# Row maxima on tiles of 128 queries that cross chunk borders, earlier queries, and another order of expert work behind the attention

## What is computed

```python
x = x + conv3x3(group_norm(x, 32), weight)              # 64 -> 64 channels, 10% of the weights are not zero
t = tokens(x)                                           # 8 x 3136 x 64
n = layer_norm(t)
q, k, v = n @ Wq.T + bq, n @ Wk.T + bk, n @ Wv.T + bv
t = t + softmax(q @ k.T / 8) @ v                        # over all 3136 keys of the image
n = layer_norm(t)
p = softmax(n @ gate_w + gate_b)                        # 16 experts
top_probs, top_idx = top_k(p, 2); top_probs /= top_probs.sum()
t = t + sum(top_probs[j] * (silu(n @ w1[e]) * (n @ w2[e])) @ w3[e] for j, e in the two chosen)
```

## Time and profile before

| | |
|---|---|
| median of 3 runs | 2943.6 us (2940.9 to 2945.2) |
| the profiled execution, its own time | 2947.36 us |
| its span, first to last instruction | 2945.6 us |
| mean granted TensorE clock | 0.958 |
| TensorE (PE) busy | 2612.0 us, 89% |
| weight loads (PEld) | 1663.2 us, 56% |
| VectorE (DVE) | 1928.1 us, 65% |
| ScalarE (ACT) | 1300.6 us, 44% |
| GpSimd (POOL) | 1020.2 us, 35% |

### The profile page before, as it was taken

The page is one execution under the profiler, slowest core; times in us unless marked ns, Lnnn a source line. Parts: engine busy times, 40 slices in busy tenths (PEclk is TensorE's granted clock), DMA queues, the critical chain, the costliest instruction groups (busy, mean ns, idle before and its releaser), DMA issues.

```text
span 2945.6 us, 47190 instructions
## 1 busy us (share of the span) xinstructions
PE 2612.0 (89%) x14013; PEld 1663.2 (56%) x14013; DVE 1928.1 (65%) x5389; ACT 1300.6 (44%) x2985; POOL 1020.2 (35%) x1093
## 2 busy tenths in 40 slices
PE   4899989999999999999999999999999999987772
PEld 2455555565656566565656656565655656554661
DVE  4577676766676676767776676767776766763432
ACT  1344444454444444454444545454444545443441
POOL 2022014200343045412452136321552136445656
PEclk8899999999999999999999999999999999997775
DMA  2133101111211122111212122111211112112332
GB/s 61 32 84 75 37 25 43 42 38 29 61 51 47 39 57 59 50 50 37 70 48 53 41 53 65 53 47 39 62 50 48 34 39 62 43 50 68 96 92 48
DMA packets 226462, 153.00 MB, mean 52 GB/s; under 512 B 100144, under 2 KB 216624, under 8 KB 226224
## 3 DMA queue, kind: packets, MB, share of 16 engines
q1 hardware_dynamic: 192112, 98.97, 12.7%
q0 software_dynamic: 31456, 48.03, 6.9%
q10 hardware_dynamic: 2656, 2.98, 0.4%
HBM read 83.92 MB, written 65.27 MB: 51 GB/s over the span
## 4 chain that ended last, share of the span: by engine, by line
PE 57%; DVE 17%; issue 7%; POOL 2%; ACT 1%; DMA 1%; SPq 1%; ACTq 0%; POOLq 0%; DVEq 0%
PE ps_o L1378 14%; PE ps_m L1341 8%; PE ps_s L1364 7%; DVE max_part L1041 5%; PE ps_s L1366 5%; PE ps_x L1522 5%; PE ps_z L1537 3%; PE ps_z L1404 3%; PE ps_z L1507 2%; PE ps_s L1522 2%; POOL got L728 2%; PE ps_y L1457 1%; PE ps_x L1530 1%; PE ps_y L1441 1%; DVE up L1196 1%
## 5 line engine op out<-in xcount | busy, mean ns | idle before, releaser
L1041 DVE TENSOR_REDUCE max_part<-ps_m 112x1 f32<-112x448 f32 x1568 | 950.7, 620 | 624.7 <-PE ps_m L1341 607.5
L886 ACT ACTIVATE prob<-ps_s 128x448 f32<-128x448 f32 x1400 | 751.7, 541 | 889.5 <-PE ps_s L1366 874.6
L1341 PE MATMUL ps_m<-k_a,q_a 128*112 128x448 f32 (+2 forms) x1792 | 611.3, 372 | 70.6 <-DVE max_part L1041 56.6
L1378 PE MATMUL ps_o<-prob,v_s 128*64 128x448 f32 x2800 | 629.6, 558 | 0.0
L1364 PE MATMUL ps_s<-q_a,k_a 128*128 128x448 f32 x1400 | 590.0, 421 | 18.6 <-issue 12.7
L707 POOL DMA_INDIRECT sorted_x<-xn,slot x448 | 433.0, 967 | 244.6 <-issue 197.5
L1366 PE MATMUL ps_s<-q_b,k_a 128*128 128x448 f32 x1400 | 512.1, 366 | 0.0
L728 POOL DMA_INDIRECT got<-sorted_y,slot x448 | 427.3, 954 | 186.4 <-issue 123.0
L746 POOL TENSOR_TENSOR ln_s<-ln_s,minus_half 112x4 f32<-112x4 f32 x56 | 57.9, 1035 | 1246.8 <-DVE ln_s L951 1086.0
L1341 PEld LDWEIGHTS ps_m<-k_a,q_a 128*112 128x112 f32 x1792 | 305.0, 177 | 280.4 <-DVE max_part L1041 162.5
L1364 PEld LDWEIGHTS ps_s<-q_a,k_a 128*128 128x128 f32 x1400 | 264.9, 189 | 208.1 <-issue 178.8
(11 more groups left out here) (184 smaller groups left out, 2944.1 us busy)
## 6 DMA issues: line engine op xcount, KB each, us to landing
fx<-sorted_x SPq DMA_DIRECT2D x43, 384.0 KB
sorted_y<-fy SPq DMA_DIRECT2D x49, 320.0 KB, 3.0
fx<-sorted_x SPq DMA_DIRECT2D x50, 256.0 KB
xh<-in_x SPq DMA_DIRECT2D x96, 126.0 KB, 2.7
sorted_x<-fy POOLq DMA_DIRECT2D x28, 320.0 KB, 6.0
sorted_x<-xn,slot POOLq DMA_INDIRECT x448
got<-sorted_y,slot POOLq DMA_INDIRECT x448
x_now<-in_x SPq DMA_DIRECT2D x112, 56.0 KB, 2.3
```

The lines of the kernel that those rows point to most:

```text
L886: a.activation(prob[(at.n * KEY_TILES + i) % PROBS][:], ps_s[(at.n * KEY_TILES + i) % 2][:, 0:CHUNK], ACT.Exp).then_inc(s["p_ready"], 1)
L1041: v.tensor_reduce(max_part[:, m % PER, m // PER:m // PER + 1], ps_m[m % 2][0:TILE, 0:CHUNK], AX.X, ALU.max).then_inc(s["max_red"], 1)
L1341: done = t.matmul(ps_m[m % 2][0:TILE, first:last], q_a[:, bass.ds(n % QUERIES, 1), j * TILE:(j + 1) * TILE].rearrange("p a c -> p (a c)"), ...
L1378: t.matmul(ps_o[side:side + CHANNELS, 0:CHUNK], v_s[u % 2][:, i, :], prob[(n * KEY_TILES + i) % PROBS][:], start=(i < 2), stop=(i >= KEY_T ...
```

## The change

1. **Maxima.** A query tile is now 128 wide. Three fit a chunk (`FULL`), and the fourth reaches over the border: the last 64 queries of an even chunk and the first 64 of the next odd one. Its seven passes run with the even chunk, so an odd chunk has 21 passes and an even one 28 (the last one's fourth tile has 64 queries): 4 x 28 + 3 x 21 = 175 for an image. The tables follow: 28 passes keep `MAXIMA`, 21 take one in each of steps 0 to 20 (`MAXIMA_FEW`), or two in steps 0 to 3 and one up to 16 in bodies with routing; there `max_total` comes at step 21, `shift` at 22. Bodies ahead of an odd chunk are those with c = 0, 2, 4.
2. **Queries** of chunk n + 2 come at step 7 in every body, since the crossing tile needs them in the same body. `q_a` gets a fourth buffer.
3. **Routing** of a group works on arrays of that group's tiles alone (28, 16, 12), and the zeros go.
4. **Behind the attention.** The body n = 56 has 50 steps: `post` and routing in the first 25 with no pairs, then the two combines at 25 and 28 and the five pairs from 26 on in the form of the later bodies. Image 7's pairs are in slices of four: 4, 4, 4, 4, 4, 2 and 4, 4, 4, 4, 2, so eleven bodies instead of nine, each with one chunk combined.

The core of the diff:

```diff
+LONE_PAIRS = 4
+GROUPS = [Group(image, 0, CHUNKS, 0, PAIRS) for image in range(BATCHES - 1)]
+GROUPS.append(Group(BATCHES - 1, 0, FIRST_PART, 0, LONE_PAIRS))
+GROUPS.append(Group(BATCHES - 1, FIRST_PART, CHUNKS - FIRST_PART, 2 * GROUPS[-1].pairs, LONE_PAIRS))
...
-COMBINE_AT_LAST, COMBINED_AT_LAST = (0, 3), (2, 5)
+COMBINE_AT_LAST, COMBINED_AT_LAST = (KEY_TILES, KEY_TILES + 3), (KEY_TILES + 2, KEY_TILES + 5)
...
-QUERIES = 3
+QUERIES, QUERIES_LOW = 4, 3
...
 MAXIMA = (1, 2, 2, 2) + 15 * (1,) + (2, 2, 2)
-MAXIMA_ROUTING = (2, 2, 2, 2, 1, 2, 1, 1, 1, 2, 1, 1, 1, 2) + 7 * (1,)
-MAX_TO = 22
+MAXIMA_FEW = 21 * (1,)
+MAXIMA_ROUTING = (2, 2, 2, 2) + 13 * (1,)
+MAX_TO, MAX_TO_FEW = 22, 21
+ASK_AT = 7
...
+def passes(n):
+
+    return BOTH + CHUNKS * (n % CHUNKS % 2 == 0)
...
+def maximum_of(n, m):
+
+    if n == 0:
+        return divmod(m, FULL + 1)
+    many = FULL * (CHUNKS - 1)
+    if m < many or passes(n) == BOTH:
+        return m // FULL, m % FULL
+    return (m - many, FULL) if m < many + CHUNKS - 1 else (CHUNKS - 1, m - many - CHUNKS + 1)
...
-        self.beside = self.n <= ALL
+        self.beside = self.n < ALL
...
-        self.ask_at = 18 if c and self.routes is None else 17
+        self.ask_at = ASK_AT
+        self.max_to = MAX_TO_FEW if passes(self.n + 1) == BOTH else MAX_TO
...
+    def steps(self):
+
+        return 2 * KEY_TILES if self.n == ALL else KEY_TILES
...
-    bodies = range(ALL + 1, TURN) if at.n < TURN else range(TURN, EXPERTS_END)
+    bodies = range(ALL, TURN) if at.n < TURN else range(TURN, EXPERTS_END)
...
             def maxima(n, u, which):
 
                 for m in which:
+                    before = passes_before(n) + m
+                    kb, j = maximum_of(n, m)
                     if m == 0:
                         pe.wait_ge(s["qa_ready"], ONE + n + 1)
+                    if j == FULL and kb == 0 and n % CHUNKS < CHUNKS - 1:
+
+                        pe.wait_ge(s["qa_ready"], ONE + n + 2)
...
-                v.tensor_tensor(picks[:, :, group.part], pick1[:, :, group.part], pick2[:, :, group.part], ALU.add)\
+                v.tensor_tensor(by_expert(b, picks), pick1[:, :, group.part], pick2[:, :, group.part], ALU.add)\
```

More of the change, by code:

```diff
@@ L138, with passes_before, queries_of @@
 LAST_GROUP = KEY_TILES // GROUP * GROUP - GROUP
-assert sum(MAXIMA) == TILES and sum(MAXIMA_ROUTING) == TILES
 assert 0 < GIVING < PER and FILLED <= KEY_TILES - OWN
-SHIFT = 23
+WIDE = 128
+FULL = CHUNK // WIDE
+BOTH = FULL * CHUNKS
+def passes(n):
+    return BOTH + CHUNKS * (n % CHUNKS % 2 == 0)
+def passes_before(n):
+    return sum(passes(k) for k in range(n))
+def maximum_of(n, m):
[5 more added lines that the diff above has]
+    return (m - many, FULL) if m < many + CHUNKS - 1 else (CHUNKS - 1, m - many - CHUNKS + 1)
+def queries_of(n, j):
+    c = n % CHUNKS
+    first = c % QUERIES * CHUNK + j * WIDE + (CHUNK - FULL * WIDE) * (c % 2)
+    return slice(first, first + (CHUNK - FULL * WIDE if c == CHUNKS - 1 and j == FULL else WIDE))
 def wait_apart(engine, sem, value):
@@ L289, in expert_steps @@
             if 0 <= k - behind < len(pairs):
-                steps.append((1 + 4 * place, name) + pairs[k - behind])
+                steps.append((at.steps() - KEY_TILES + 1 + 4 * place, name) + pairs[k - behind])
     return steps
@@ L882, in body @@
                 experts = expert_steps(at)
-                for i in range(KEY_TILES):
+                for i in range(at.steps()):
                     if at.attends:
@@ L1250, in body @@
                         next_queries(at.n + 2)
-                    if i == MAX_TO and at.ahead:
+                    if i == at.max_to and at.ahead:
                         max_total(at.n + 1)
@@ L1311, in _ @@
                     next_queries(place - 1)
+                reduces(0, block[3:4])
                 if place < CHUNKS:
@@ L1348, in shift @@
                 pe.wait_ge(s["maxneg_ready"], ONE + n + 1)
-                for j in range(PER):
-                    last = t.transpose(ps_y[:, j * TILE:(j + 1) * TILE],
-                                       max_neg[:, j:j + 1].to_broadcast([TILE, 128]), ident[0:TILE, 0:TILE])
+                part = CHUNK - FULL * WIDE
+                full = [(j, slice(0, WIDE)) for j in range(FULL)]
+                tiles = [(FULL, slice(WIDE - part, WIDE))] + [(FULL + 1 + j, here) for j, here in full] if n % CHUNKS % 2 \
+                    else full + [(FULL, slice(0, part))]
+                first = 0
+                for j, here in tiles:
+                    many = here.stop - here.start
+                    last = t.transpose(ps_y[:, first:first + many], max_neg[here, j:j + 1].to_broadcast([many, 128]), ident[here, here])
+                    first += many
                 last.then_inc(s["shiftT_done"], 1)
@@ L1479, in variance, with routed @@
                     t.matmul(ps_y[:, 1:2], pair_mean[:], gn_e[:], start=True, stop=True).then_inc(s["gn_var_done"], 1)
-            flat_picks = picks[:].rearrange("p e t -> p (e t)")
+            def routed(b, weights):
+                many = EXPERTS * GROUPS[b].tiles
+                return t.matmul(ps_y[0:TILE, 0:many], weights[:], picks[:].rearrange("p e t -> p (e t)")[:, 0:many], start=True, stop=True)
             def route_total(b):
```

121 lines of the change are left out of this document (65 added, 56 removed).

## The result

The changed kernel takes 2900.7 us, the median of 4 runs (2893.4 to 2906.9), against 2944.4 for the kernel before beside it: ratio 0.985, 95% interval 0.982 to 0.988. The forecast was 2868.6 with a range up to 2900, so the direction was right and the size was not: 44 us instead of 75. The experiments ran in four batches, each on a chip of its own and beside the kernel before: e1 to e4 (2943.3 us for the kernel before), a0 and e5 to e7 (3258.7), a1 and f1 to f3 (2943.4), g1 to g4 (2944.6).

The account below looks back on a forecast made before the run. TensorE was taken to set the pace, VectorE holding it up in places. Passes -64 and queries -5, times 0.9, gave -62; with the tail's -13, -75 off the 2943.6 median gave 2868.6 us, own range 2850 to 2885, with near rivals 2840 to 2900.

Parts of the forecast that it names:

- Passes of c = 0, 2, 4: Seven passes fewer in bodies of chunks 0, 2, 4: -4.0, -2.4, -2.1 us, 8.5 an image, -64 in all.
- weight loads cost nothing: Passes loading 128 instead of 112 weight columns: put at nothing, since streaming paces; 18 us if that cover were gone.
- Queries at step 7: Query work moved from step 18 (17): nothing on TensorE, about 0.2 us gained in chunks 1, 3, 5, 6, -5 in all.
- The upper bound of +14 us: Worst case for the queries' move: 54 bodies each 0.25 us late at turned2, nothing gained at step 20.
- The shift: Row-maxima transposes: 64-row pieces not costed; a second reduce under 0.2 us in eight bodies put at nothing.
- Lead-in: First image's start: one pass in four moves behind tokens and queries; put at nothing.
- Tail: Routing and pairs behind the attention: earlier slots, 24 gathers left instead of 40; -14, taken as -13 us.
- signs of being wrong: Chunk 0 body gaining under 2 us, attention clock under 0.97, or more than 32 gathers left behind the pairs.
- signs of being right: Among them: image stretch 335 to about 325 us, chunk 0 4 us shorter, 2 and 4 by 2 to 2.5, others under 0.5.
- TensorE alone paces: Rival: every VectorE wait that goes reappears at hid, xn or the POOL norms; 2904 us (2890 to 2912), chance 0.16.
- The rival of the clock: Rival: missing passes leave gaps, the clock is lowered for longer, kernel slower; 2950 to 2980 us, middle 2960, chance 0.03.

Follow-up runs that it names:

- e1: Kernel before with only the queries moved to step 7 in every body: 2961.4 us against 2943.3, ratio 1.007.
- e4: Changed kernel with the lead-in's fourth passes ahead of turned keys and statistics as before, except where chunk 1's queries are needed: 2891.4 us, ratio 0.983.
- a0: Changed kernel itself again, unaltered, as control on the slow chip: ratio 1.005 to the kernel before.
- e5: Changed kernel with each shift made by four equal 128-row transposes, no 64-row piece, on the slow chip: ratio 1.004 to the kernel before.
- e7: Changed kernel with old lead-in order, four equal transposes per shift, and double passes of steps 19 and 20 at 6 and 14; slow chip, ratio 0.998.
- a1: Changed kernel itself again, unaltered, as control of its batch: 2899.7 us, ratio 0.985 to the kernel before.
- f1: Changed kernel with each shift made by four equal 128-row transposes, no 64-row piece: 2889.2 us, ratio 0.982, beside a control of 2899.7.
- f3: Changed kernel with double passes of steps 19, 20 at 9, 13, last expert codes at step 23, equal-transpose shift, old lead-in order: 2853.3 us, ratio 0.970.
- g1: Kernel before with the double passes of steps 19 and 20 moved to 9 and 13, queries still at step 18: 2938.0 us, ratio 0.998.
- g4: f3 with tables per body: c = 1, 5, 6 move only step 20's double, to 9; first image as in the changed kernel: 2864.2 us, ratio 0.974.
- e3: Changed kernel with the old order behind the attention, image 7's pairs in slices of five: 2912.9 us, ratio 0.989.

## Why the prediction was right and wrong

- **Passes of c = 0, 2, 4**: forecast -4.0, -2.4, -2.1, measured -3.35, -2.26, -2.03, in spite of a shift that cost 0.1 to 0.25 more. Right, body by body. That weight loads cost nothing here was right as well: step 9 takes 2.35 or 2.36 us with either width.
- **Queries at step 7**: forecast -0.2 us in each of c = 1, 3, 5, 6, -5 in all; alone it measured +18. This is the step that failed. The forecast counted q_b on VectorE and took "TensorE's part is the same work elsewhere: nothing". e1 shows +0.6, +0.7, +0.3 and +0.8 in these bodies. The work was the cover of VectorE's reduce, and q_b's leaving step 20 gained nothing there (3.38 us both times). The upper bound of +14 us came from the 0.25 us at turned2. In the changed kernel turned2 waits 1.2 to 1.4 us for q_b in ten bodies of images 1 and 2 (in image 1 of before 0.6 to 0.9 us for the tokens), and 0.2 us in four later ones; the bound is still below the 18 measured.
- **The shift**: never costed, that is, put at nothing without a reason. The forecast weighed only the width of a weight load in the passes; the 64-row transposes in the diff cost about 10 us (f1).
- **Lead-in**: forecast at nothing, "in work that is there anyway". It cost 5.4 us, and the old order gives back 4.4 (e4's trace): the one pass in four had filled part of the wait for the normalised values, which grew from 1.64 to 4.25 us.
- **Tail**: forecast -13; the stretch behind the last score is 13.0 shorter, and undoing it costs 12 to 13 (e3). POOL, then DVE and PE, in the tail of the changed kernel, against the earlier trace rows:

```profile
2679.15 1.14 POOL L765 DMA_INDIRECT got<-sorted_y,slot  x1 [16.87 <-DVE t_out L1269]
2689.27 0.96 POOL L744 DMA_INDIRECT sorted_x<-xn,slot  x1 [0.30 <-issue]
...
2726.82 0.95 POOL L765 DMA_INDIRECT got<-sorted_y,slot  x1 [7.85 <-DMA sorted_y<-fy]
...
2859.20 0.98 POOL L765 DMA_INDIRECT got<-sorted_y,slot  x1 [3.01 <-DMA sorted_y<-fy]
...
2888.28 0.93 POOL L765 DMA_INDIRECT got<-sorted_y,slot  x1 [0.30 <-issue]
```

```profile
2662.39 0.43 DVE L1126 TENSOR_TENSOR ln_c<-ln_c,ln_s 112x256 f32<-112x256 f32 x1 [7.90 <-POOL ln_s L783]
...
2663.75 0.98 PE L1513 MATMUL ps_y<-ident,xn 112*128 112x112 f32 x4 [12.60 <-DVE xn L1129]
...
2723.17 0.39 PE L1573 MATMUL ps_z<-ident,k_a 128*128 128x128 f32 x2
...
2849.21 0.63 PE L1573 MATMUL ps_z<-ident,k_a 128*128 128x128 f32 x2
```

  As forecast, the tokens still wait for POOL (its ln_s), the gather stands ahead of the scatters, and 24 gathers are left behind the last pair's store ((2888.28 - 2859.20) / 1.24 + 1). The pairs of image 7 take 126.0 us from first to last fx instead of 115.1, 10.9 more and not 5.3. It came out even: from the last score to their first fx 77.5 us instead of 84.8, from their last fx to the end 50.1 instead of 66.7.
- **The sum.** Lead-in +5.4, images 1 and 2 -6.5, images 3 to 7 -18.7, image 8 -13.5, tail -13.0: -46 between the two profiled spans, of -75 forecast. Queries (23 away from the forecast), shift (10) and lead-in (5) come to 38 us, more than the 29 that are missing here; image 8 gained 4 us more than the 9 forecast, and the rest is not accounted for. None of the forecast's signs of being wrong came up; of its signs of being right, the image's stretch of 325 us and the other bodies within 0.5 us did not. The rival "TensorE alone paces" gave 2904 with 0.16, close to the measured time, but not for its reason: the bodies that lost passes gained nearly what was forecast. The rival of the clock saw a real effect, at two places, and neither its sign nor its size: the mean granted clock in the image's stretch stayed at 0.99, and at c = 3 it fell in the kernel before too.

## What to carry to other kernels

Work on an engine that is moved away costs what it covered: before moving it, look at what the next instruction behind it waits for, on another engine. Where a diff puts a 64-row matmul among 128-row ones, count a stop at each change, or pad it to one form. And read every kind of body of a loop, not three of seven: c = 3, with the largest single fault, 17 to 20 us for one number in a table, was in no row of the forecast.

## What was unexpected of the hardware

- A 64-row transpose behind 128-row ones leaves the weight load 0.17 us idle and delays the next score by 0.26 us (0.64 against 0.38 in f1). A 112-row one beside 128-row scores did not (0.32 before).
- TensorE's clock fell from 1.00 to 0.50 behind waits of 1.53 and 1.89 us, in image 1, and behind two of 1.74 and 1.23, and stayed at 1.00 behind one of 0.91 or 1.36. Behind a wait of 1.22 or 1.23, among the same instructions, it fell in the changed kernel and stayed in e4, so the length of the wait does not decide it alone; what else does is open. The falls shown lasted about 6 us; eight weigh matmuls took 3.26 us in one instead of 1.72.
- The same change has the ratio 0.985 in the result and on another batch's chip, and 1.005 on the slow chip, whose mean granted clock is 0.90 instead of 0.96. Why was not settled.
